# Graph attention passes: a gather per tile with copies per unit, and each edge sum as two 64-column products

## What is computed

```python
def gatv2_layer(x, src, dst, Wl, Wr, att, bias, n_nodes, heads):
    xl = (x @ Wl).reshape(N, heads, Dh)
    xr = (x @ Wr).reshape(N, heads, Dh)
    e = jax.nn.leaky_relu(xl[src] + xr[dst], NEG_SLOPE)
    logits = jnp.einsum('ehd,hd->eh', e, att)
    m = jax.ops.segment_max(logits, dst, num_segments=n_nodes)
    a = jnp.exp(logits - m[dst])
    denom = jax.ops.segment_sum(a, dst, num_segments=n_nodes)
    alpha = a / denom[dst]
    out = jax.ops.segment_sum(alpha[:, :, None] * xl[src], dst, num_segments=n_nodes)
    return out.mean(axis=1) + bias
```

## Time and profile before

| | |
|---|---|
| time, 3 runs | 4051.95, 4058.42, 4059.17 us; median 4058.42 |
| span of the profiled execution | 4048.7 us |
| time of the profiled execution | not listed apart; the median lies 9.7 us above this span |
| edge pass of layer 1 | chunk 0 starts at 198.5 us, chunk 3 at 286.8, chunk 44 at 1737.8 |
| edge pass of layer 2 | chunk 0 starts at 2095.2 us, chunk 44 at 3416.3 |

### The profile page before, as it was taken

One profiled execution on the slowest core, in us unless ns is written; L12 is line 12 of the kernel. 1 busy time (PEld: TensorE's weight loads), 2 busy tenths in 40 slices (PEclk: granted clock), 3 DMA queues, 4 the chain that ended last, 5 costly groups with the idle time before them and its releaser, 6 DMA issues. The chain is left out here.

```text
span 4048.7 us, 76266 instructions
## 1 busy us (share of the span) xinstructions
PE 3293.6 (81%) x24199; PEld 2204.4 (54%) x24199; DVE 2807.3 (69%) x6887; ACT 1717.6 (42%) x3696; POOL 2796.9 (69%) x2157
## 2 busy tenths in 40 slices
PE   0399999999999999996339977777777777568986
PEld 0246666666666666674226655554455555346763
DVE  3558888888888888886537755565555555579972
ACT  3254444444444444432215433333333333147861
POOL 4488888888777777505678888888888885537630
PEclk9999999999999999986669988888888888569997
DMA  2233343343333333323114433333333332211210
GB/s 58 51 65 80 86 88 86 86 89 85 80 87 86 86 85 88 75 54 83 48 36 79 91 74 67 68 69 67 67 68 73 69 68 48 52 26 40 44 34 28
DMA packets 607173, 274.68 MB, mean 68 GB/s; under 512 B 445801, under 2 KB 568077, under 8 KB 606260
## 3 DMA queue, kind: packets, MB, share of 16 engines
q1 hardware_dynamic: 261848, 102.14, 11.7%
q0 software_dynamic: 107328, 77.78, 11.1%
q10 hardware_dynamic: 237600, 89.88, 9.1%
HBM read 161.25 MB, written 105.94 MB: 66 GB/s over the span
## 5 line engine op out<-in xcount | busy, mean ns | idle before, releaser
L901 PE MATMUL L_e_ps_z<-L_e_xT,L_w_abs 128*128 128x500 f32 x2700 | 1501.4, 642 | 0.0
L826 POOL DMA_INDIRECT L_e_xs<-in_x_dram,src_idx x880 | 1193.1, 1356 | 335.4 <-issue 261.4
L826 POOL DMA_INDIRECT L_e_xs<-x_d,src_idx x820 | 1079.7, 1317 | 253.3 <-issue 249.8
L952 PEld LDWEIGHTS L_e_ps_v<-L_e_xs,L_e_p 125*128 125x128 f32 x5400 | 860.0, 204 | 628.3 <-issue 569.6
L996 ACT ACTIVATE L_e_rl<-L_e_ps_z 128x500 f32<-128x500 f32 x1350 | 793.0, 587 | 883.0 <-PE L_e_ps_z L901 883.0
L952 PE MATMUL L_e_ps_v<-L_e_xs,L_e_p 125*128 125x65 f32 x5400 | 796.2, 274 | 11.1 <-DVE L_e_acc L1180 9.4
L1180 DVE SCALAR_TENSOR_TENSOR L_e_acc<-L_e_acc,L_e_row,L_e_ps_v 128x130 f32<-128x130 f32 (+1 forms) x1440 | 448.5, 311 | 424.1 <-PE L_e_ps_v L952 281.4
L888 PE MATMUL L_e_ps_x<-ident,L_e_xs 125*64 125x125 f32 x1800 | 288.7, 285 | 310.7 <-DMA L_e_xs<-x_d,src_idx 251.8
L989 ACT ACTIVATE L_e_xT<-L_e_ps_x 128x500 f32<-128x500 f32 x450 | 264.3, 587 | 619.3 <-PE L_e_ps_x L891 590.4
L901 PEld LDWEIGHTS L_e_ps_z<-L_e_xT,L_w_abs 128*128 128x128 f32 x2700 | 427.4, 198 | 77.8 <-issue 24.3
L1163 DVE TENSOR_TENSOR L_e_p<-L_e_ohc,L_e_ae 125x640 f32<-125x640 f32 x540 | 427.1, 818 | 0.0
(11 more groups left out here) (304 smaller groups left out, 3620.2 us busy)
## 6 DMA issues: line engine op xcount, KB each, us to landing
L_v_d<-L_e_acc ACTq DMA_DIRECT2D x225, 260.0 KB
L_e_dlb<-dloc_d SPq DMA_DIRECT2D x90, 468.8 KB, 4.9
L_v_d<-L_e_acc ACTq DMA_DIRECT2D x225, 130.0 KB
L_e_xw<-x_d SPq DMA_DIRECT2D x1800, 12.0 KB
L_e_xs<-in_x_dram,src_idx POOLq DMA_INDIRECT x900
L_e_xs<-x_d,src_idx POOLq DMA_INDIRECT x900
L_e_lim<-limits_d SPq DMA_DIRECT2D x180, 39.1 KB
L_max_d<-L_e_me SPq DMA_DIRECT2D x45, 78.1 KB
```

Source lines behind the costliest of these rows:

```text
L826: pool.indirect_dma_start(xs[c.slot(XR)][:, n, 0:D], None, lay.x_rows, bass.IndirectOffsetOnAxis(k.src_idx[:, u:u + 1], 0)).then_inc(gath[ ...
L901: pe.matmul(ps_z[part % ZR][:, 0:QT], lay.w_abs[:, part * 128:(part + 1) * 128], xT[q][:], start=True, stop=True).then_inc(s["z_ready"], 1)
L952: ins = pe.matmul(ps_v[u // 2 % 2][:, u % 2 * VX + v * XW:u % 2 * VX + (v + 1) * XW], p[st % 3][:, u % NQ, v, :, :].rearrange("e n h -> e ...
```

## The change

**Rows.** POOL gathers each of the 800 tiles once, into a new ring `tiles` of 64 tiles in SBUF, in groups of 16. SP then issues one copy per unit from `tiles` to `xs` (SBUF to SBUF, 125 rows of 256 bytes), at a place in the ring that it loads into a register. Semaphores `fetched_to` (groups landed, raised by POOL after the fourth gather of the next group), `copied` (chunks copied, raised by SP) and `freed` tie the two. The indices of windows and tiles of 20 units are loaded into 20 registers at once. Layer 1 has chunk 0 copied and 32 tiles gathered before the edge pass, layer 2 chunks 0 to 2 and 64 tiles. `xs` has 6 chunks in both layers. In layer 1 the buffers of `dlb` and `limits` go from 3 to 2.

**Sums.** Each product of `sums` becomes two with 64 stationary columns, at output partitions 0 and 64; the four units' sums stand together ahead of `project`.

**Setup.** Of the 9 gathers of `src` blocks 2 are left. `src` is also loaded by tile and transposed on PE, and two more lists of 900 numbers are stored.

```diff
+def fetch_tiles(k, pool, lay, f0, f1):
+    for f in range(f0, f1):
+        if f >= RF:
...
+            pool.wait_ge(lay.copied, copies[(f - RF) % 16])
+            pool.sem_inc(lay.freed, 1)
+        for i in range(TF):
+            g = f * TF + i
+            pool.indirect_dma_start(lay.tiles[:, g % TR * D:(g % TR + 1) * D], None, lay.x_rows,
+                                    bass.IndirectOffsetOnAxis(k.src_tile[:, g:g + 1], 0)).then_inc(lay.gath[f % RF], 16)
+            if i == 3 and f > f0:
+                tiles_there(pool, lay, f - 1)
+    tiles_there(pool, lay, f1 - 1)
...
+def load_rows(k, sp, lay, c):
+    places = listed(sp, lay, c, 1, (TR - 1) * D)
+    sp.wait_ge(lay.fetched_to, counts(sp, f"{lay.nm}need{c.number}_", lay.lists[c.slot(2)][0:1, 2, CU - 1:CU])[0])
+    for n, at in enumerate(places):
+        sp.dma_start(lay.xs[c.slot(XR)][:, n, 0:D], lay.tiles[:, bass.ds(at, D)]).then_inc(lay.ld_r[c.slot(XR)], 16)
+
+def serve(k, sp, lay, c):
+    sp.wait_ge(lay.ld_w[c.slot(2)], c.uses(2) * 16)
+    load_windows(k, sp, lay, c)
+    if c.after(1):
+        rows_there(sp, lay, c.back(1))
+    load_rows(k, sp, lay, c)
+    if c.back(-1).there():
+        list_units(k, sp, lay, c.back(-1))
...
-                        pe.wait_ge(gath[r], c.uses(XR) * GB)
+                        pe.wait_ge(ld_r[r], c.uses(XR) * GB)
...
                     for v in range(HV):
-                        ins = pe.matmul(ps_v[u // 2 % 2][:, u % 2 * VX + v * XW:u % 2 * VX + (v + 1) * XW],
-                                        p[st % 3][:, u % NQ, v, :, :].rearrange("e n h -> e (n h)"),
-                                        xs[c.slot(XR)][:, u, :], start=True, stop=True)
+                        for half in range(2):
+                            ins = pe.matmul(ps_v[u // 2 % 2][64 * half:64 * half + 64, u % 2 * VX + v * XW:u % 2 * VX + (v + 1) * XW],
+                                            p[st % 3][:, u % NQ, v, WN // 2 * half:WN // 2 * (half + 1), :].rearrange("e n h -> e (n h)"),
+                                            xs[c.slot(XR)][:, u, :], start=True, stop=True)
...
-                    for part in range(4):
-                        if part % (4 // C) == 0 and (c.after(1) or q >= 1) and zc.there():
-                            project(zc, zq, part // (4 // C))
-                        if c.after(3) and bc.there():
-                            sums(bc, bq, part)
+                    if c.after(3) and bc.there():
+                        for n in range(Q):
+                            sums(bc, bq, n)
+                    if (c.after(1) or q >= 1) and zc.there():
+                        for part in range(C):
+                            project(zc, zq, part)
```

219 lines of the change are left out of this document (138 added, 81 removed).

## The result

The changed kernel takes 4638.57 us (median of 4 runs, 4617.76 to 4669.67), the kernel before beside it 4058.80 us. The ratio is 1.1435, with a 95% interval of 1.1388 to 1.1483: 14% slower. The forecast was 3873 us, and the range ended at 4010. The profiled execution has a span of 4667.9 us.

The account below looks back on a forecast made before the run. PE was taken to bound layer 1, POOL layer 2. Setup -9, layer 1 start +22, sums -96 and layer 2 -102 gave -185 us: span 4048.7 to 3864, 3873 on the median's scale; range 3835 to 4010 (80%).

Parts of the forecast that it names:

- The bound in both layers: PE bounds layer 1 at 35.4 us a chunk, POOL's gathers bound layer 2 at 32.2 us a chunk.
- Part 1, the sums: PE, layer 1: 64-column halves run together, a quad 0.94 us instead of 1.56; chunk 33.05 us, -96 us over 41 chunks.
- the width change: PE, sums block: one more change of tile width an iteration, taken at 0.15 us, with ends 0.05 and 0.30.
- The wait for DVE's chain: PE, layer 1: third sum's new wait for DVE falls on the quad before; cost nothing, 41 us if 1 us a chunk.
- halves in turn: Rival, PE's sums: each half waits for the other, 1.89 us a quad; time 4067 us, no change; 11%.
- the rule that I had cited: PE's sums: loads overlap products only in different row groups; each half pays both, iteration 9.1 us, time about 4385; 1%.
- Part 3, the copies on SP: SP, 40 transfers a chunk at 0.36 to 0.45 us, 14 to 18 us beside 2.5 of the rest: hidden under 28.9.
- Part 2, the gathers: POOL, 17.8 gathers a chunk: 28.9 us in layer 2 at 1.62 each; 29.5 in layer 1 at 1.66, under PE's 33.05.
- Part 4, the ends: Setup -9 us, layer 1 start +22 us, layer 2's chunk 44 starting at 3314 instead of 3416, -102 us.
- a late `dlb`: SP: `dlb` stands behind the tile wait and 20 copies, delaying DVE, then PE; while PE has slack only the ends move.
- Few DMA engines: Rival: each copy's rows go to five engines; from 41 ns a row the gain is cancelled, at 45 ns 4207 us; 8%.
- Order on SP and DVE comes through: Rival: group waits, late `dlb` or clock drops cost; layer 1 at 34.3, layer 2 at 30.0 us a chunk, 3969 us; 18%.

Follow-up runs that it names:

- e5: Kernel before with both changes of the sums, its edge-pass gathers left out once every buffer of `xs` was filled: 3681.95 us beside 4092.96.
- e11: Changed kernel with the sums of before, SP's copies left out once each buffer of `xs` was filled, gathers kept: 4088.78 us beside 4085.44.
- e6: Kernel before with both changes of the sums; after the first chunks POOL issues 20 plain 125-row transfers a chunk instead of gathers: 3673.47 us beside 4092.96.
- e7: Kernel before with both changes of the sums; after the first chunks SP issues 20 plain 125-row transfers a chunk, POOL no gathers: 3901.75 us beside 4092.96.
- e13: As e6, with each plain transfer on POOL split in three, 60 a chunk, to keep POOL busy: 3969.76 us beside 4085.44 for the kernel before.
- e8: Changed kernel with gathers of tiles left out from the fifth group on, copies and semaphores kept: 4242.99 us beside 4092.96 for the kernel before.
- e1: Kernel before with both changes of the sums and none of the rows, 20 gathers a chunk on POOL: 4399.62 us beside 4090.06, ratio 1.075.
- e3: Kernel before with only the order changed, the four units' sums together ahead of `project`, still 128 columns: 4204.36 us beside 4090.06, ratio 1.029.
- e14: Kernel before with both changes of the sums, plus a small POOL memset ahead of each layer 1 gather: 4029.16 us beside 4047.35, ratio 0.996.
- e15: Kernel before with both changes of the sums, plus a POOL wait for PE ahead of every fourth layer 1 gather: 4026.66 us beside 4047.35, ratio 0.995.
- e18: Kernel before, unchanged, run once more on one chip with e16 and e17: 4069.94 us beside 4077.77.
- e16: e1 unchanged, run again on one chip with e17 and e18: 4381.76 us beside 4077.77 for the kernel before, ratio 1.073.
- e9: Kernel before, unchanged, run again for its trace: 4036.89 us beside 4045.30.
- e17: e14 unchanged, run again on one chip with e16 and e18: 4359.40 us beside 4077.77 for the kernel before, ratio 1.071.
- e12: Kernel before with both changes of the sums, each gather from chunk 6 on fetching 32 rows instead of 125: 5241.41 us beside 4085.44.
- e4: Kernel before with only each product of the sums cut into two of 64 columns, old order: 4164.72 us beside 4090.06, ratio 1.018.

## Why the prediction was wrong

**The bound in both layers: right**, for PE in layer 1 and POOL in layer 2. e5's and e11's rates follow from it.

**Part 1, the sums: right in the mechanism; the chunk's number is luck in part.** 16 pairs took 1.11 us against 1.09, 0.069 a pair against 0.059, and the width change is inside it. The chunk is 33.15 us against 33.05, in four kernels (e5, e6, e7, e13). But two errors cancel in it. The sum took off 7.08 - 6.61 = 0.47 us an iteration, and undisturbed each of the five loses 0.69 to 0.70 us (7.40 to 6.70, for one): the last unit's sums ahead of `reduce` had cost 0.49 and not 0.39, and three of the new records already run among the products of `turn`. That gives 31.9. The wait for DVE's chain, which the forecast cost at nothing, gives back 1.26. The halves run together. The rival *halves in turn* (1.89) is refuted. So, for this shape, is the rule that I had cited from the Trainium skill, "TensorE: Matmul & The Clock Gate", Part 3, "The mechanism", that a weight load overlaps a running product only where the row groups differ. Both halves use all rows, by it a pair takes some 0.22 us (an estimate, twice 0.049 + 0.059), and the trace disagrees with 0.069. The same section also lets a load run ahead into a background weight buffer; whether that happens here no run shows.

**Part 3, the copies on SP: the first step that failed.** I priced 40 transfers at 0.36 to 0.45 us each, "with the load gone". A window transfer is 0.55 and a copy 0.84, 27.7 us for the 40. The rest of the lap is 34.8 - 27.7 = 7.1 and not 2.5, of which some 4 are the two gaps with the register loads, which the sum had put at nothing. So SP needs 33.8 to 34.8 us a chunk instead of 16.5 to 20.5, and is the bound of both layers by itself: over PE's 33.05, over POOL's 28.9. My own last line named the condition, "if copies take SP more than 29 us a chunk". The upper bound stood in the earlier trace rows: 0.82 for a transfer at a place from a register, taken as it is, gives 40 x 0.82 + 2.5 = 35.3 us, near what came. The agreement is partly chance: the windows got cheaper with their loads gone, and the loads in bulk and the list took up what that saved. I had subtracted a register load that I had not seen separately, then gone towards the store of 0.26, whose place is fixed. The rows nearest in form were the 20 windows. e8 sizes this failure: +94 us against the forecast in layer 1 and +226 up to the end of layer 2, with 29 at the start. With the 28 behind, which go with where it ran and not with the copies, these are 377 of the 804.

**What no row of before showed: the second step.** I counted on PE's signals to arrive with its work. In the changed kernel 68% are late. With the new sums alone layer 1 goes from 33.15 to 43.17 us a chunk (e5, e1). The kernel before runs at 35.39 or 35.45 with 0 or 21% of them late. That a late signal finds slack there, behind a PE that always has work queued in layer 1 and a POOL that is the bound in layer 2, and that the change took this slack away, is argued and not shown. e3 speaks against slack alone: its PE has more to do than before (36.2 us a chunk undisturbed), and it still loses 2.4 us a chunk, with 50% late. The other 804 - 377 = 427 us of the miss are what gathers add to e8 (across two places, so the size is rough). In layer 1 the two causes don't add: 43.17 with late signals alone, 35.34 with SP alone, 43.43 with both. There SP waits for DVE, which waits for PE's signals, in 1000 to 1500:

```profile
SPq L947 <- DVE L_e_falls L1249: 105.6, 6, 22.2
```

105.6 us in 11.5 chunks are 9.2 a chunk, and 34.8 + 9.2 = 44.0. SP has no slack to catch up, since its lap already takes longer than PE's. In layer 2 SP decides: 33.78 without gathers, 35.05 with; and e1, with 75% of its layer 2 increments late but SP free, keeps 30.54.

**Part 2, the gathers: right in layer 2, and hidden.** e11, where copies are absent, has 29.18 us a chunk in layer 2 against 28.9. In layer 1 the price was a little low: 1.72 us a gather in e14 and e15, against 1.66.

**Part 4, the ends: partly.** The setup saved 4.7 us and not 9 (the first tile gather at 132.6 against 137.3). The mechanism of a late `dlb` was right and too cheap: already in chunks 1 to 3 SP's lap is 35 us, and DVE waits 52.1 us for `dlb` between 200 and 345, 43.0 in one piece:

```profile
DVE L_e_oht L1174 <- DMA L_e_dlb<-dloc_d: 52.1, 3, 43.0
```

**The rivals.** *Few DMA engines*: the split was there, the price not. The transfers of a copy land within 0.43 to 0.51 us, and a packet of its queue takes 18.4 ns (packets of 256 bytes, alone), so 125 x 18.4 / 480 = 4.8 run at a time, an estimate: five engines, as "DMA: Bandwidth & Descriptors", "Why a DMA increments its semaphore by 16 and not by 1", in the Trainium skill, has it for 125 rows; the trace agrees. At 18.4 ns that is 2500 x 18.4 / 5 = 9.2 us a chunk, well under the 41 ns that the rival needed. The queue as a whole now moves

```profile
q1 hardware_dynamic: 498838, 160.20, 15.6%
```

which is 23 ns a packet, less than the 29 of the earlier trace rows. *Order on SP and DVE comes through* had the right place (SP's order, `dlb` late, once a chunk in e8) and a price of 96 us. One of its signs did come, `L1054` waiting for the chain, at 1.26 us a chunk in e5; it did not have SP itself as the bound. No rival did. That is why the range failed to hold the time: each of SP's prices was varied for latency and none for the sum.

**What stays open.** Even with signals on time the changed kernel would be slower than before: e8, which has none late, has a span of 4241, and less the 28 us of its tail some 4213. That is an estimate, since no run of the changed kernel has its signals on time. Not settled are: how a gather holds up PE's increments; what differs between one place or hour and another; and why grouped or halved sums raise the share of late ones (0.21 in e18, 0.71 in e16, same place). Where the changed kernel ran is itself open: the kernel before took 4052 to 4061 us beside it, between the 4037 to 4049 us of the blocks with signals on time (e9, e14) and the 4070 to 4101 of the others, and yet 68% of its increments are late. The only versions that beat both kernels are the new sums with a pause on POOL, or with a wait that never held it (e14, e15), by 0.4 to 0.5% where signals are on time; POOL's 34.5 us a chunk leaves the sums no more than that. e17 takes 1.07 where they are late. I would not ship it.

## What to carry to other kernels

Add up a queue's issue time like an engine's busy time before moving work onto it, and price an instruction by the row nearest in form as it stands (a register address, SBUF as source), not by that row less something that wasn't seen apart. When a bound is lifted, ask what it had been hiding: a wait "remote" or "issue" of several microseconds, with the producer's record long over, says to look at when the semaphore moved. A cure is shown only when the uncured twin ran beside it, and when the trace shows that the cure did anything at all.

## What the runs showed of the hardware that I had not expected

- In some places PE's semaphore increments reach other engines 0.6 to over 20 us late while POOL carries out gathers. Never behind the last gather (e5, e8), never with plain transfers on POOL even at 93% busy (e13), and worse with shorter gathers (e12: 0.88 us each, layer 1 at 50.9 us a chunk). The records of the products look on time all the while. That fits the Trainium skill, "Perfetto Trace Analysis", "Tensor Engine Instruction (MATMUL, LD_WEIGHTS)": a product's end in the profile is an estimate from its size, and the semaphore's propagation lies behind it. What delays it stays open.
- SP needs 0.84 us for a copy of 125 rows from SBUF at a place from a register with its two register instructions (0.70 alone), 0.55 for a window of 96 rows from DRAM at such a place, and 0.42 for 125 rows from DRAM at a fixed place (e7). Whether the source in SBUF or the register makes the larger part was not tried apart.
- A pair of 64-column products costs 0.069 us in a block of sixteen pairs, against 0.098 for one of 128 columns. Between wide products eight of the narrow ones take 0.39 us like the four before, and the wide one ahead of them 1.03 instead of 0.90 us (e4).
